# Rotary attention of a two-layer block: output transposes ahead of the second scores, the keys' row exchange behind the second maxima, and a maximum split made of one-axis reductions

## What is computed

```python
h = rms_norm(x, norm_weight)
q, k, v = split(h @ w_qkv.T)          # 16 heads of 64
q = apply_rope(q); k = apply_rope(k)  # t*cos + rotate_half(t)*sin
k = concat([pm, k]); v = concat([pm, v])   # 4 persistent rows in front
scores = where(causal, q @ k.T * dim_head**-0.5, min)
out = softmax(scores) @ v
return merge_heads(out) @ w_out.T
```

## Time and profile before

| | |
|---|---|
| median of 3 runs | 3835.32 us (3834.57 to 3835.72) |
| profiled execution | 3842.36 us, span 3840.4 us |
| PE busy in the span | 3163.6 us (82%) |
| DVE busy | 2258.7 us (59%) |
| ACT busy | 1695.6 us (44%) |
| POOL busy | 1211.7 us (32%) |

### The profile page before, as it was taken

The page is one execution under the profiler, slowest core; times in us unless marked ns, Lnnn a source line. Parts: engine busy times, 40 slices in busy tenths (PEclk is TensorE's granted clock), DMA queues, the critical chain, the costliest instruction groups (busy, mean ns, idle before and its releaser), DMA issues. The chain is left out here.

```text
span 3840.4 us, 143685 instructions
## 1 busy us (share of the span) xinstructions
PE 3163.6 (82%) x58952; PEld 2402.2 (63%) x58952; DVE 2258.7 (59%) x6772; ACT 1695.6 (44%) x5164; POOL 1211.7 (32%) x1528
## 2 busy tenths in 40 slices
PE   8677488988889888489985899999999889999571
PEld 5445188888888888445532566666666567777451
DVE  4667644444444444368865888889888845555232
ACT  2179333333333333257743555565555534444230
POOL 0032410000000000033310655565555544444332
PEclk9899755555555555589997999999999955555786
DMA  4011100000000000010001000000000010110336
GB/s 132 1 55 46 31 25 14 25 14 14 25 14 25 14 14 25 13 34 21 20 1 52 2 3 3 2 3 3 2 3 2 16 50 31 33 33 28 109 97 173
DMA packets 112984, 116.09 MB, mean 30 GB/s; under 512 B 55041, under 2 KB 96458, under 8 KB 112371
## 3 DMA queue, kind: packets, MB, share of 16 engines
q1 hardware_dynamic: 104674, 87.36, 8.0%
q0 software_dynamic: 7824, 21.46, 1.5%
HBM read 79.65 MB, written 29.13 MB: 28 GB/s over the span
## 5 line engine op out<-in xcount | busy, mean ns | idle before, releaser
L676 PE MATMUL banks<-hp,whp 128*128 128x8 f16 x24576 | 741.4, 168 | 118.3 <-DVE hp L743 118.3
L676 PEld LDWEIGHTS banks<-hp,whp 128*128 128x128 f16 x24576 | 697.7, 104 | 179.1 <-DVE hp L743 170.2
L709 ACT ACTIVATE ig<-banks 128x32 f32<-128x32 f32 x512 | 101.4, 198 | 576.8 <-PE banks L676 576.8
L738 DVE SCALAR_TENSOR_TENSOR carry<-ig 128x16 f32<-128x16 f32 x512 | 92.1, 180 | 425.4 <-ACT ig L709 425.4
L646 POOL COPY HT<-hist 128x128 f32 x64 | 21.3, 408 | 987.0 <-DVE hp L748 987.0
L1747 PE MATMUL rnn_banks<-rnn_hp,rnn_whp 128*128 128x8 f16 x6144 | 285.6, 171 | 41.1 <-ACT rnn_hp L1805 15.6
L1747 PEld LDWEIGHTS rnn_banks<-rnn_hp,rnn_whp 128*128 128x128 f16 x6144 | 247.8, 107 | 108.3 <-ACT rnn_hp L1805 76.6
L1088 ACT ACTIVATE att_PH<-att_stp 128x1024 f16<-128x1024 f32 (+3 forms) x258 | 183.4, 711 | 296.6 <-PE att_stp L888 296.6
L1147 POOL TENSOR_TENSOR att_QK<-att_rot,att_QK 128x512 f16<-128x512 f32 x133 | 187.4, 1409 | 244.1 <-ACT att_QK L1080 244.1
L654 PE MATMUL banks<-xs,wxp 128*128 128x64 f16 x3168 | 263.7, 241 | 0.0
L1007 DVE TENSOR_TENSOR att_PL<-att_P,att_PH 128x1024 f16<-128x1024 f32 (+3 forms) x257 | 236.0, 957 | 0.5 <-issue 0.2
(11 more groups left out here) (595 smaller groups left out, 7767.1 us busy)
## 6 DMA issues: line engine op xcount, KB each, us to landing
gen_w<-in_L_cond_W_dram SPq DMA_DIRECT2D x32, 512.0 KB
exp_xt<-expert_rows_scratch SPq DMA_DIRECT2D x80, 129.0 KB
edge_cb<-cols_scratch SPq DMA_DIRECT2D x16, 512.0 KB, 3.7
XT<-expert_found_scratch SPq DMA_DIRECT2D x16, 512.0 KB, 5.0
mod_xn<-in_x_dram SPq DMA_DIRECT2D x8, 512.0 KB
XT<-in_xT_dram SPq DMA_DIRECT2D x1, 4096.0 KB
out_dram<-exp_ob SPq DMA_DIRECT2D x64, 64.0 KB, 2.2
attw_st<-in_L_attn_w_qkvT_dram SPq DMA_DIRECT2D x6, 512.0 KB
```

The source lines that it names most:

```text
L676: last=nc.tensor.matmul(out, whp[:,wpart,k,col:col+128], hp[:,k,hpart], start=False,stop=True,skip_group_check=True)
```

## The change

Three things, with the functions they are in:

1. On PE in the rotary slot, turn_outputs (the four transposes) moves from behind the second scores to ahead of them.
2. On DVE, rotate is taken apart for the rotary stage into by_cosines (the old L979) and swap_rows (the old L980). For the queries they stay together; for the keys, swap_rows moves behind the second maxima.
3. The maximum split, in both stages, uses tensor_reduce only. The maxima are kept as such and the sign moves into the scale of ACT's copy. Tile 3's two maxima are joined by a reduction of a small tile; high part, minus the high part, and low part (a sum of the two) are three reductions. That is four instructions for three in the rotary stage and three for two in the plain stage.

```diff
-        mx=sb("mx",[P,2,5]); mparts=sb("mparts",[P,QT,P],BF16)
+        mx=sb("mx",[P,2,QT,2]); mlast=sb("mlast",[P,2,2]); mparts=sb("mparts",[P,QT,P],BF16)
...
                 project(it,2*(s+2)+1)
+                if s>=1: turn_outputs(it,s-1)
                 if s>=-1: scores(it,s+1,1)
-                if s>=1: turn_outputs(it,s-1)
                 if s>=0: scores_T(it,s,1)
...
+            def by_cosines(it,j):
+                if j: dve.wait_ge(summed,it*2*S+j)
+                dve.wait_ge(proj,it*2*S+j+1)
+                nc.vector.tensor_tensor(ab[:,0],pj[:,:],c_.tab[:,0],ALU.mult)
+            def swap_rows(it,j):
+                nc.vector.stream_shuffle(ab[:,1],pj[:,:],[i^1 for i in range(32)]).then_inc(evac,1)
...
             def split_max(it,n):
-                base=(it*S+n)*(2 if rope else 1)
+                base=(it*S+n)*(3 if rope else 2)
                 dve.wait_ge(maxed,it*S*NG+n*NG+NG)
                 if rope:
-                    nc.vector.tensor_tensor(mx[:,:,3:4],mx[:,:,3:4],mx[:,:,4:5],ALU.max).then_inc(m_step,1)
+                    nc.vector.tensor_reduce(out=mx[:,:,QT-1,0:1],in_=mlast[:,:,:],axis=X_AX,op=ALU.max).then_inc(m_step,1)
                     dve.wait_ge(m_step,base+1)
                 if n: dve.wait_ge(m_turned,it*S+n)
...
-                nc.vector.tensor_scalar(hi_,mx[:,:,0:4],-1.0,None,ALU.mult).then_inc(m_step,1)
+                nc.vector.tensor_reduce(out=hi_,in_=mx[:,:,:,0:1],axis=X_AX,op=ALU.max).then_inc(m_step,1)
                 dve.wait_ge(m_step,base+(2 if rope else 1))
-                nc.vector.scalar_tensor_tensor(out=lo_,in0=mx[:,:,0:4],scalar=-1.0,in1=hi_,op0=ALU.mult,op1=ALU.subtract).then_inc(m_ready,1)
+                nc.vector.tensor_reduce(out=mx[:,:,:,1:2],in_=hi_,axis=X_AX,op=ALU.max,negate=True).then_inc(m_step,1)
+                dve.wait_ge(m_step,base+(3 if rope else 2))
+                with nc.allow_low_precision(reason="the low part of a maximum in two parts"):
+                    nc.vector.tensor_reduce(out=lo_,in_=mx[:,:,:,:],axis=X_AX,op=ALU.add).then_inc(m_ready,1)
...
-                rotate(it,2*(s+2))
+                by_cosines(it,2*(s+2)); swap_rows(it,2*(s+2))
                 if s>=1: normalise(it,s-1)
                 if s>=-1: low_values(it,s+1); maxima(it,s+1,0)
-                rotate(it,2*(s+2)+1)
+                by_cosines(it,2*(s+2)+1)
                 if s>=-1: maxima(it,s+1,1)
+                swap_rows(it,2*(s+2)+1)
                 if s>=1: low_outputs(it,s-1)
...
-                nc.scalar.activation(mT[:,:],mtp[:,0:T],ACT.Copy).then_inc(m_copied,1)
+                nc.scalar.activation(mT[:,:],mtp[:,0:T],ACT.Copy,scale=-1.0).then_inc(m_copied,1)
```

More of the change, by code:

```diff
@@ L975, in rotate @@
                 n,what=divmod(j,2)
[L976 to L984, removed]
+                if j>1: dve.wait_ge(lo,it*2*S+j-1)
+                dve.wait_ge(proj,it*2*S+j+1)
+                nc.vector.tensor_scalar(rot_of(j),pj[:,:],c_.bias(batch(it,n),what,n%NP_),c_.gate(batch(it,n),n%NP_),ALU.add,ALU.mult).then_inc(evac,1)
+            def by_cosines(it,j):
+                if j: dve.wait_ge(summed,it*2*S+j)
+                dve.wait_ge(proj,it*2*S+j+1)
+                nc.vector.tensor_tensor(ab[:,0],pj[:,:],c_.tab[:,0],ALU.mult)
+            def swap_rows(it,j):
+                nc.vector.stream_shuffle(ab[:,1],pj[:,:],[i^1 for i in range(32)]).then_inc(evac,1)
             def maxima(it,n,g):
@@ L989, in maxima @@
                     w_=min(key_columns(qt),T)
-                    i=nc.vector.tensor_reduce(out=mx[:,:,qt:qt+1],in_=s_ps[:,:,at:at+w_],axis=X_AX,op=ALU.max); at+=w_
-                if rope and GROUPS[g]==(QT-2,): i=nc.vector.tensor_reduce(out=mx[:,:,4:5],in_=s_ps[:,:,at:at+PM],axis=X_AX,op=ALU.max)
+                    top=mlast[:,:,0:1] if rope and qt==QT-1 else mx[:,:,qt,0:1]
+                    i=nc.vector.tensor_reduce(out=top,in_=s_ps[:,:,at:at+w_],axis=X_AX,op=ALU.max); at+=w_
+                if rope and GROUPS[g]==(QT-2,): i=nc.vector.tensor_reduce(out=mlast[:,:,1:2],in_=s_ps[:,:,at:at+PM],axis=X_AX,op=ALU.max)
                 i.then_inc(maxed,1)
             def split_max(it,n):
-                base=(it*S+n)*(2 if rope else 1)
+                base=(it*S+n)*(3 if rope else 2)
                 dve.wait_ge(maxed,it*S*NG+n*NG+NG)
                 if rope:
-                    nc.vector.tensor_tensor(mx[:,:,3:4],mx[:,:,3:4],mx[:,:,4:5],ALU.max).then_inc(m_step,1)
+                    nc.vector.tensor_reduce(out=mx[:,:,QT-1,0:1],in_=mlast[:,:,:],axis=X_AX,op=ALU.max).then_inc(m_step,1)
                     dve.wait_ge(m_step,base+1)
                 if n: dve.wait_ge(m_turned,it*S+n)
-                hi_,lo_=[mparts[:,:,:].rearrange("p q (h d) -> p h q d",h=2)[:,:,:,part] for part in range(2)]
-                nc.vector.tensor_scalar(hi_,mx[:,:,0:4],-1.0,None,ALU.mult).then_inc(m_step,1)
+                hi_,lo_=[mparts[:,:,:].rearrange("p q (h d) -> p h q d",h=2)[:,:,:,part:part+1] for part in range(2)]
+                nc.vector.tensor_reduce(out=hi_,in_=mx[:,:,:,0:1],axis=X_AX,op=ALU.max).then_inc(m_step,1)
                 dve.wait_ge(m_step,base+(2 if rope else 1))
-                nc.vector.scalar_tensor_tensor(out=lo_,in0=mx[:,:,0:4],scalar=-1.0,in1=hi_,op0=ALU.mult,op1=ALU.subtract).then_inc(m_ready,1)
+                nc.vector.tensor_reduce(out=mx[:,:,:,1:2],in_=hi_,axis=X_AX,op=ALU.max,negate=True).then_inc(m_step,1)
+                dve.wait_ge(m_step,base+(3 if rope else 2))
+                with nc.allow_low_precision(reason="the low part of a maximum in two parts"):
+                    nc.vector.tensor_reduce(out=lo_,in_=mx[:,:,:,:],axis=X_AX,op=ALU.add).then_inc(m_ready,1)
             def low_weights(it,n,t):
```

## The result

The changed kernel takes 3929.05 us (median of 4 runs, 3924.09 to 3931.0), the kernel before 3834.95 in the same session. The ratio is 1.0245, with a 95% interval of 1.0229 to 1.026. The profiled execution took 3924.09 us, with a span of 3922.1. The prediction was 3927.

What follows compares the result with a forecast made beforehand. PE bounds the kernel before, DVE with POOL the changed one: 48 slots x 1.74 = 83.5, token slots +4, output slots 0, ramp +1, plain attention +3, together +92 us, so 3927 us. Range 3850 to 3960.

Steps and rivals of the forecast that it cites:

- (a): Transposes ahead of the second scores on PE: +0.33 us a slot with PE as bound, nothing with DVE as bound.
- (b): Later keys' shuffle on DVE: POOL's sine multiplication of the keys then holds the first low-weights subtraction, +0.85 us.
- (c): POOL's queries subtraction, having waited, runs between the two low-weights subtractions and holds the second: +0.82 us.
- rival (1): Only the later shuffle holds DVE; POOL's queries subtraction loses both times, DVE isn't the bound: 3856 us, chance 10 in 100.
- (d): The split on DVE: join of the last maxima no longer held, -1.05 us; one added instruction, +0.22 us.
- (e): POOL's subtraction for the keys holds one of two DVE instructions behind the later pair's first: +0.97 us.
- (f): DVE-POOL chain from the queries' cosines to the next slot's start: fixed 4.20 us, giving a slot of 14.65 us.
- The output slots: The 7 rotary slots with the output projection, where DVE idles 9.93 us waiting for PE: 0 added.
- The plain attention: Stage ahead of the rotary one: split has three instructions instead of two, 17 times 0.2, +3 us.
- PE's share: Sign in the profile after: PE's busy share in the rotary stage near 84%.
- The wait for the second maximum: Sign on PE: waits for low weights and for the DVE-POOL chain take its place.
- rival (5): Lengthening feeds on itself through less busy PE, lower granted clock and more holds: above 3960 us, chance 2 in 100.

Runs made afterwards that it cites:

- e5: Changed kernel with the transposes put back behind the second scores, the later shuffle and the new split kept: 3925.06 us, ratio 1.023.
- e9: Changed kernel with POOL's subtraction for the low part of the queries cut to 8 of 512 columns in the rotary stage: 3840.13 us, ratio 1.0011.
- e2: Kernel before with only the transposes moved ahead of the second scores: 3793.14 us, ratio 0.9981.
- e7: Changed kernel with POOL's sine multiplication of the keys cut to 8 of 512 columns: 3843.81 us, ratio 1.0017.
- e1: Kernel before with only the keys' shuffle moved behind the second maxima: 3879.67 us, ratio 1.0206.
- e3: Kernel before with only the new maximum split by reductions: 3813.07 us, ratio 1.0033.
- f2: Kernel before with transposes ahead of second scores, value projection ahead of third scores, low outputs ahead of second maxima: 3871.03 us, ratio 1.0082.
- f4: f2 with POOL's low part of the keys after the query sum and ACT's memory-keys copy before its queries copy, old split: 3821.49 us, ratio 0.9949.
- e8: Kernel before with POOL's sine multiplication of the keys cut to 8 of 512 columns: 3826.72 us, ratio 0.9972.
- f3: f4 with the new maximum split by reductions instead of the old one: 3824.9 us, ratio 0.9965.
- e4: Changed kernel with the keys' shuffle put back behind the cosine multiplication, transposes ahead and new split kept: 3817.91 us, ratio 1.0045.

## Why the prediction was right, step by step

**(a)** The transposes cost nothing with DVE as the bound: right, e5. The +0.33 with PE as the bound was too much: in e9, where PE is the bound, the slot is 0.20 longer. With the shuffle in its old place the transposes gain 8 us in the token slots (e2), a case that the prediction didn't work out.

**(b) and (c)** Right. The first pair ends at D+6.55; 6.54 was worked out. POOL's L1152 wins against the second L1011 since it has asked for 1 us. The Trainium skill's rule ("SBUF — State Buffer", section on the two separate sides), whoever starts first has the pair of ports for the whole instruction, agrees: pairs of 3.78 with two of POOL's instructions on them, 3.05 with one (e7), 2.82 with one whole and one short (e9). One reading was off: by rows 4, 5 and 8 the first L1147 came 0.11 us before the first L1007 ended (2417.50 and 1.22 against 2418.61), not 0.08. And it lost in 31 of the 48 normal slots only, not in all, as rival (1) takes it; the slot of rows 4 was one of the 31.

**(d)** The size holds, the reason doesn't. The added step costs 0.2 us as taken: the pair behind the split starts at D+8.25 in e1 and at D+8.44 in the change. But e1 shows L997 free with the old split, so the 1.05 belongs to the delay in (b) and (c), which puts L997 behind POOL's instruction. In the whole change the two can't be told apart by the sum; that it came out the same is luck. Alone, the split costs 12 us (e3), about half of it through a new hold.

**(e) and (f)** Right: the queries' cosines at D+10.44 (10.45), then 4.21 (4.20), a slot of 14.65. Of the 56 slots 34 lie between 14.65 and 14.67; most of the others are those with a lower clock and the ones right behind them (below).

**Terms of the sum that were mis-sized.** The 56 slots give +89.2 (87.5 worked out, with the token slots), the ramp -0.1 instead of +1. The output slots, put at 0, give +3.6, nearly all in two of them: 25.99 and 26.1 us where the other five take 24.3 to 24.7 (below). The plain attention, put at +3, gives +0.3: from its first to its last scores 286.6 us before, 286.9 after. Why the third instruction of its split costs nothing there is open. Together that is +93.0 where 91.5 was worked out, because the errors of the output slots and of the plain attention nearly cancel, which is luck. What is left of the 94.1 is less than the parts behind the stage vary from one execution to the next.

**The signs** that the prediction listed came in the main. The split's first step is never held:

```profile
L998 DVE TENSOR_REDUCE att_mx<-att_mlast x65: 158/159/161, 2122.3 to 3132.7; 128x2 f32<-128x4 f32 x65
```

PE's share is 86.7% rather than 84; the lower clock isn't the reason, since e5 at a granted clock of 1.00 has 87.2% (778.09 of the same 892 us). The pair shows 3.78 in one row of two instructions, so the 2.1 us of the first can't be read by itself. The wait for the second maximum, said to be replaced, is still there (35.0 us in 49 waits), and costs nothing now, because PE is not the bound. Part 1 makes it longer: without it, in e5, this wait is 16.7 us.

## What to carry to other kernels

An instruction is moved with all that it releases: the shuffle itself cost nothing in its new place, but it released POOL 0.95 us later, onto work of DVE that shares its ports. So write down, for each POOL instruction that reads SBUF, which two-input DVE instruction lies under it, and move POOL's order together with DVE's (f2 and f4 differ by 1.3% so). At such a place 0.1 us more or less decides over a hold of 1 us, so a part that looks neutral can lose or gain, and each part should be run alone.

## What the runs showed of the hardware that was not expected

**Who gets the ports.** When POOL is ready while a two-input instruction of DVE runs and another such one stands right behind, a few hundredths decide. In rows 4 and 5 POOL's L1147 is ready 0.11 us before the first L1007 ends (after its 1.22 us alone) and loses; so it does in the 31 slots of before, at 0.10 or 0.11. In the other 17 slots it is ready 0.18 us before, or more, and wins. In e3 it wins at 0.15, and the closest case is in e8, at 0.14, here DVE's row and then POOL's:

```profile
2444.88 3.06 DVE L1007 TENSOR_TENSOR att_PL<-att_P,att_PH 128x1024 f16<-128x1024 f32 x2
```

```profile
2445.96 1.16 POOL L1148 TENSOR_TENSOR att_QK<-att_rot,att_QK 128x512 f16<-128x512 f32 x1 [2.22 <-ACT att_QK L1080]
```

Between 0.11 and 0.14 no run lies. These figures leave out the slots in which the first of the pair was itself held.

**A reduction is not held.** Reductions from SBUF ran in the midst of POOL's instructions at full speed; in f3 40 of them lay wholly within one. POOL's and DVE's rows of one place there:

```profile
2998.00 1.26 POOL L1147 TENSOR_TENSOR att_rot<-att_ab 128x512 f32<-128x512 f32 x1
```

```profile
2998.19 0.16 DVE L998 TENSOR_REDUCE att_mx<-att_mlast 128x2 f32<-128x4 f32 x1
2998.38 0.19 DVE L1002 TENSOR_REDUCE att_mparts<-att_mx 128x8 bf16<-128x8 f32 x1
```

L997, of the same size with two inputs, took 1.21 under POOL. The prediction had left this open. So the new split does what its form suggests; it only met no hold to avoid in the changed kernel.

**The clock.** Before, PE had a mean granted clock of 1.00 over the stretch from 2143 to 3035 us. After, it is 0.98. In 12 slots of that stretch PE has a short dip to the lower level, 1.2 GHz. Two of them are the long output slots. The windows of after show the first of them, and one of the other ten (the granted clock is the 0.93 and the 0.88):

```profile
2373.44:2399.43 25.99, 23.96 (x265) 13.32 (x261) 13.28 (x26) 8.13 (x17) 7.35 (x6) 0.93 0.01 4
```

```profile
2329.46:2343.92 14.46, 12.94 (x213) 9.19 (x210) 13.21 (x25) 7.79 (x16) 11.04 (x8) 0.88 0.01 3
```

In the output slot PE had waited 2.03 us for L1028, where that of before waits 1.2. The twelve matmuls behind then took 4.26 us, and 2.75 in an output slot of before. PE's rows of after, then of before:

```profile
2376.36 1.69 PE L915 MATMUL att_vo<-att_ao,att_wo 128*128 128x512 f16 x6 [2.03 <-DVE att_ao L1028]
2377.84 4.26 PE L915 MATMUL att_pj<-att_ao,att_wo 128*128 128x512 f16 x12
```

```profile
2471.78 2.75 PE L915 MATMUL att_pj<-att_ao,att_wo 128*128 128x512 f16 x12
```

A mean of 0.93 over 26 us is 1.8 us of clock lost, and the slot exceeds the shortest output slots by 1.7. What a dip costs depends on the bound. In the ten slots without the output projection, where DVE is the bound, the cost is next to nothing: such a slot takes 14.44 to 14.49 us and the next one mostly 14.87, which is 29.33 against 29.32 for two slots without a dip (three next ones, just ahead of an output slot, take 15.1). In e4, where DVE waits for PE at D, it is 1.5 us in each of four slots.

What brings the clock down is not shown. It can't be the wait alone: all 7 output slots of after have one of 2.0 (13.8 us in 7 waits), and two of them are long. In e7, with the same waits (13.0 us in 7), there are again two, of 25.99 us; in e1, e5 and e9, where they are 1.5 to 1.6 at most, the stage has no dip; in e4 they are up to 2.0 and no output slot has one. In the prediction this was rival (5) on a small scale: it came, at 3.6 us, and did not feed on itself.
